# The slot tables AT, AT_FIRST and AT_LAST of a four-layer kernel laid anew

## The reference

```python
def reference(x, ...):                    # x: (16, 256, 256) float32
    # layer 0: gradients and Laplacian of each 256x256 plane with grid coefficients, an Euler step, relu
    x = _L0_cond_ref(x, A_grid, B_grid, dt)
    # layer 1: adapter 256->64, gelu, a 64x64 matrix chosen by the sequence's id, 64->256, residual, layer norm
    hidden = gelu(x @ down_W.T + down_b)
    hidden = hidden @ expert_W[id].T + expert_b[id] + domain_emb[id]
    x = layer_norm(hidden @ up_W.T + up_b + x) * ln_gamma + ln_beta
    # layer 2: scale and shift from a small network of t; norm over the whole plane, silu, 256x256 product, twice
    h = silu(noise_encoding(t) @ W1 + b1) @ W2 + b2
    scale, shift = h @ Wsc + bsc, h @ Wsh + bsh
    out = silu(scale * plane_norm(x) + shift) @ W_in + b_in
    x = silu(scale * plane_norm(out) + shift) @ W_out + b_out + x
    # layer 3: adaptive layer norm, attention of 16 heads of width 16 with bias and mask, MLP 256->1024->256
    x = ln(x) * (1 + scale3) + shift3
    probs = softmax(mask(q @ k.T / 4 + attention_bias))
    x = x + (probs @ v) @ Wo + bo
    return x + gelu2(ln(x) * g2 + beta2) @ W1 + b1) @ W2 + b2
```

## Time and profile before

| What | us |
|---|---|
| median of 3 runs | 923.07 (922.08 to 923.43) |
| the profiled execution | 923.14 |
| its span, first to last instruction | 921.10 |
| front of pair 0, until the first exponential | 84.31 |
| turn of pair 0 | 95.85 |
| turns of pairs 1 to 6, each | 104.44 to 104.79 |
| turn of pair 7 | 81.68 |
| after the start of the last head's exponential | 31.84 |

### The profile page before, as it was taken

One profiled execution on the slowest core, in us unless ns is written; L12 is line 12 of the kernel. 1 busy time (PEld: TensorE's weight loads), 2 busy tenths in 40 slices (PEclk: granted clock), 3 DMA queues, 4 the chain that ended last, 5 costly groups with the idle time before them and its releaser, 6 DMA issues.

```text
span 921.1 us, 18266 instructions
## 1 busy us (share of the span) xinstructions
PE 859.3 (93%) x5712; PEld 665.7 (72%) x5797; DVE 740.4 (80%) x2371; ACT 729.5 (79%) x1904; POOL 236.6 (26%) x236
## 2 busy tenths in 40 slices
PE   9876979999999999999999999999999999999987
PEld 8564657777777777777777777777777777777666
DVE  8767798888898888788898898788898898865542
ACT  2134879889798879979798878979798888977763
POOL 2232223332222313332123323232132323120000
PEclk9996999999999999999999999999999999999999
DMA  9827473744456453744446462744446452646400
GB/s 258 237 69 185 142 192 93 196 121 117 136 155 164 134 156 98 208 122 125 138 143 157 137 166 82 194 143 138 133 131 172 118 165 91 189 133 168 142 12 23
DMA packets 133082, 130.90 MB, mean 142 GB/s; under 512 B 18265, under 2 KB 123481, under 8 KB 132969
## 3 DMA queue, kind: packets, MB, share of 16 engines
q1 hardware_dynamic: 101616, 112.02, 42.9%
q10 hardware_dynamic: 31370, 17.71, 6.9%
HBM read 112.61 MB, written 17.07 MB: 141 GB/s over the span
## 4 chain that ended last, share of the span: by engine, by line
PE 57%; ACT 20%; DVE 8%; issue 3%; POOL 0%; ACTq 0%; DVEq 0%
PE ff_ps L1368 11%; PE ff_ps L1349 8%; PE PT_ps L1404 7%; ACT Pr L1083 5%; PE G L1154 5%; PE scores_ps L1389 4%; PE G L1146 4%; PE ctx_ps L1426 3%; DVE bias L928 3%; ACT L1083 3%; PE scores_ps L1386 2%; ACT ffT L1069 2%; ACT tanh L1065 2%; PE ff_ps L1335 2%; ACT PT L1096 2%
## 5 line engine op out<-in xcount | busy, mean ns | idle before, releaser
L1083 ACT ACTIVATE Pr<-bias,nmax 128x256 f32<-128x256 f32 x512 | 255.8, 506 | 35.3 <-DVE nmax L928 34.6
L928 DVE CUSTOM_DVE_ANT_0 bias<-scores_ps,bias 128x256 f32<-128x256 f32 x512 | 194.0, 419 | 48.2 <-PE scores_ps L1389 26.7
L1096 ACT ACTIVATE PT<-PT_ps 128x512 f32<-128x512 f32 x256 | 152.4, 596 | 50.9 <-PE PT_ps L1404 46.3
L1404 PE MATMUL PT_ps<-ident,Pr 128*128 128x128 f32 x1024 | 156.0, 274 | 7.8 <-ACT Pr L1083 7.8
L566 POOL TENSOR_TENSOR rstd<-var,half_neg 128x2 f32<-128x2 f32 (+1 forms) x64 | 43.4, 678 | 388.6 <-DVE var L691 244.5
L1404 PEld LDWEIGHTS PT_ps<-ident,Pr 128*128 128x128 f32 x1024 | 119.9, 141 | 16.6 <-ACT Pr L1083 13.0
L1349 PE MATMUL ff_ps<-ctxT,w 128*128 128x256 f32 x480 | 117.2, 387 | 13.0 <-ACT ffT L1069 10.7
L1368 PE MATMUL ff_ps<-w,ffT 128*128 128x256 f32 x480 | 113.1, 381 | 0.3 <-DVE ffT L905 0.3
L1349 PEld LDWEIGHTS ff_ps<-ctxT,w 128*128 128x128 f32 x480 | 86.3, 190 | 33.0 <-ACT ffT L1069 16.3
L1389 PE MATMUL scores_ps<-k_stack,q_stack 96*128 96x256 bf16 x512 | 99.3, 275 | 6.1 <-issue 2.1
L1083 ACT ACTIVATION_READ_ACCUMULATOR Pr<-bias,nmax 128x1 f32 x512 | 100.5, 196 | 0.0
(11 more groups left out here) (223 smaller groups left out, 1649.0 us busy)
## 6 DMA issues: line engine op xcount, KB each, us to landing
bias<-in_fside_Bx16xSxS_dram SPq DMA_DIRECT2D x256, 256.0 KB, 3.2
part_dram<-front ACTq DMA_DIRECT2D x32, 384.0 KB, 2.8
q_stack<-part_dram SPq DMA_DIRECT2D x32, 192.0 KB, 3.8
k_stack<-part_dram SPq DMA_DIRECT2D x32, 192.0 KB, 3.7
F<-in_x_dram SPq DMA_DIRECT2D x16, 256.0 KB, 3.7
ada<-rows_dram SPq DMA_DIRECT2D x16, 256.0 KB, 4.6
q_stack<-part_dram SPq DMA_DIRECT2D x32, 128.0 KB, 3.7
k_stack<-part_dram SPq DMA_DIRECT2D x32, 128.0 KB, 3.7
```

The costliest lines, as they stand in the source:

```text
L928: nc.vector.tensor_tensor_reduce(out=t, in0=SP_[:, n % 2, q * S:(q + 1) * S], in1=t, scale=-1.0, scalar=BIG, op0=ALU.add, op1=ALU.min, acc ...
L1083: ins = nc.scalar.activation(Pr[:, n % PR, q, :], bias[:, n // CH % RING, 2 * (n % CH) + q, :], ACT.Exp, bias=nmax[:, n, q:q + 1], scale=-1.0,
L1096: nc.scalar.activation(PT[:, m % BATCH, :, :].rearrange("p c q -> p (c q)"), TP[:, m % 2, :], ACT.Identity).then_inc(pt_ok, 1)
L1404: ins = pe.transpose(TP[:, m % 2, c * S + q * P:c * S + (q + 1) * P], Pr[:, m % PR, q, c * P:(c + 1) * P], ident[:, :])
```

## The change

The three tables get other numbers. No instruction is added, taken out or moved to another engine, and the loops, waits and warming products stay as they are; SP's queue is the same row by row. Most numbers of `AT` move by 0.25 to 2 slots; those of `AT_FIRST` and `AT_LAST` by up to 32. A line or two of each table:

```diff
 AT
-      "wo": (21.75, 37.25), ... "w1": ((25, 26.25, 28, 29.75), (41.75, 42.75, 43, 45.75)),
+      "wo": (21.75, 38.75), ... "w1": ((25, 26.75, 28.5, 29), (42, 43.5, 43.75, 45.75)),
-      "k_out": (28, 41.75), "v": (28.75, 46), "V": (29, 46.5), "mask": (20, 2)}
+      "kf": (25, 40.75), "k_split": (26.75, 42), "k_out": (26.5, 43.25), "v": (28.75, 43.5), "V": (30, 45.75),
 AT_FIRST
-AT_FIRST = {"s_gelu": (3.25, 3.25), ... "s_sel": (2, 2), ... "l0": (4, 8.75),
+AT_FIRST = {"s_gelu": (10.5, 10.5), ... "s_sel": (1.5, 1.5), ... "l0": (1, 11.5),
 AT_LAST
-           "w2": ((31.25, 37, 47, 48.25), (67, 73.25, 75.75, 77.5)), "out": (55.25, 70), "store": (57, 68.75)}
+           "w2": ((37.25, 40.75, 42.25, 49), (67.5, 82.25, 84.75, 90.75)), "out": (69.25, 90.75),
```

More of the change, by code:

```diff
@@ L72 @@
            "masks": 0}
-AT = {"x4": (27.75, 46.25), "ctx_spread": (19.5, 40.5), "ctx": (19.75, 36.25), "ctx_scale": (19.5, 36.25),
[4 rows of a table removed]
-      "out": (35, 51.25), "store": (36.75, 57.5), "prods_p": (0.5, 18.75), "prods": (0.75, 14), "diffs": (2, 16.5),
[8 rows of a table removed]
-      "q_split": (25.5, 40.25), "q_out": (25.25, 42), "k": (25.5, 41), "kf": (25, 40.5), "k_split": (26.75, 41.75),
-      "k_out": (28, 41.75), "v": (28.75, 46), "V": (29, 46.5), "mask": (20, 2)}
-AT_FIRST = {"s_gelu": (3.25, 3.25), "s_sin": (0.25, 0.25), "s_se": (2.75, 2.75), "s_trig": (3.5, 3.5), "s_onehot": (4, 4),
-            "s_grid": (4.25, 4.25), "s_h1": (3, 3), "s_h2": (3.5, 3.5), "s_h2t": (3.75, 3.75), "s_sel": (2, 2),
-            "s_cond": (4.5, 4.5), "s_condt": (6.25, 6.25), "s_mask": (24.25, 24.25), "s_rows": (15.25, 15.25),
-            "x4": (28, 46.75), "s_fill": (4.25, 4.25), "s_bq": (7.75, 7.75), "s_w2": (34.25, 34.25),
-            "prods_p": (0.25, 5.5), "prods": (5.5, 6), "diffs": (5.5, 6.5), "edges": (5.5, 6.5), "l0": (4, 8.75),
-            "x1": (5.75, 12), "relu": (4.25, 7), "x1_turn": (4.75, 16.5), "x1T": (5, 7.25), "res1": (5.75, 13.75),
-            "down": (6.25, 16.75), "hid": (5.75, 7.5), "expert": (6.5, 17.5), "expT": (6.5, 7.75), "up": (8.5, 18),
[7 rows of a table removed]
@@ L103 @@
-AT_LAST = {"ctx_spread": (23.25, 35.25), "ctx": (20.5, 41.25), "ctx_scale": (20.5, 38.5), "wo": (22, 46),
[4 rows of a table removed]
-           "w2": ((31.25, 37, 47, 48.25), (67, 73.25, 75.75, 77.5)), "out": (55.25, 70), "store": (57, 68.75)}
+AT = {"x4": (28.25, 51.5), "ctx_spread": (21.25, 35.5), "ctx": (20.75, 37.5), "ctx_scale": (20, 37.25),
[4 rows of a table added]
+      "w2": ((30.5, 31.5, 33.5, 35.25), (46.25, 47.75, 49.5, 51.5)), "out": (35.5, 51.75), "store": (37.25, 62),
+      "prods_p": (0.75, 20), "prods": (1.5, 13.25), "diffs": (3, 16.5), "edges": (3.25, 16.75), "l0": (5, 18.25),
+      "x1": (5.75, 18.75), "relu": (5.75, 18.75), "x1_turn": (7, 20.5), "x1T": (6, 19), "res1": (6.5, 27),
+      "down": (8.5, 21.5), "hid": (8.25, 20.5), "expert": (9.75, 21.75), "expT": (8.75, 20.5), "up": (10, 22),
[7 rows of a table added]
+      "mask": (20, 2)}
@@ new lines @@
+AT_FIRST = {"s_gelu": (10.5, 10.5), "s_sin": (0.5, 0.5), "s_se": (2.75, 2.75), "s_trig": (0.25, 0.25),
+            "s_onehot": (2.25, 2.25), "s_grid": (2.25, 2.25), "s_h1": (2, 2), "s_h2": (2, 2), "s_h2t": (2.5, 2.5),
+            "s_sel": (1.5, 1.5), "s_cond": (3.5, 3.5), "s_condt": (7.5, 7.5), "s_mask": (21.5, 21.5),
+            "s_rows": (13, 13), "x4": (21, 44), "s_fill": (7.25, 7.25), "s_bq": (24, 24), "s_w2": (35.25, 35.25),
+            "prods_p": (0.75, 0.75), "prods": (3.75, 6.25), "diffs": (3.75, 6.25), "edges": (4.5, 7.25),
+            "l0": (1, 11.5), "x1": (5.25, 12.5), "relu": (3, 6.25), "x1_turn": (3.5, 12.75), "x1T": (3.5, 11.5),
+            "res1": (0.75, 5.25), "down": (8, 13.75), "hid": (4, 17), "expert": (8, 14.75), "expT": (5, 18.25),
[8 rows of a table added]
@@ L109 @@
+AT_LAST = {"ctx_spread": (18, 37.75), "ctx": (21.25, 34.75), "ctx_scale": (21.25, 43.25), "wo": (22, 38),
[5 rows of a table added]
+           "store": (58.25, 94.25)}
 SP_AT = {"front": (0, 7), "stacks": (1, 2, 9, 11), "mask": 6, "rows": (12, 3)}
```

## The result

The changed kernel takes 931.8 us (median of 10 runs, 926.8 to 935.6), the kernel before 923.1 (10 runs beside it). The ratio is 1.0079, with a 95% interval of 1.0051 to 1.0107: it is slower by 0.8%, where 917.3 and faster was forecast. The profiled execution took 931.08 us with a span of 929.1, which is 8.0 longer than the span before; between the medians it is 8.7.

| stage | before | after | change | forecast |
|---|---|---|---|---|
| front of pair 0 | 84.31 | 93.85 | +9.54 | +7.7 |
| turn of pair 0 | 95.85 | 100.45 | +4.60 | -2.8 |
| turns of pairs 1 to 6 | 627.42 | 621.91 | -5.51 | -10.2 |
| turn of pair 7 | 81.68 | 77.88 | -3.80 | -1.0 |
| end | 31.84 | 35.01 | +3.17 | +0.5 |

What follows compares the result with a forecast made beforehand. PE was taken to bound the six steady turns, and a step-by-step sequence across engines the front of pair 0. Front +7.7, turn 0 -2.8, steady -10.2, turn 7 -1.0, end +0.5: -5.8, so 923.1 becomes 917.3 us (range 909 to 930).

Steps and rivals of the forecast that it cites:

- (D): Front of pair 0: after idling, PE runs `l0` at the low clock, 3.1 us more, total 920.4; chance 0.12.
- the slack at `xs`: Front of pair 0: `xs` waited for DVE after `up`, so 2.45 us of the 10.2 delay is taken up.
- paid on the path: Front of pair 0: the first gelu table's load of 1.28 us now follows the wait of `hid`, delaying the first sequence.
- The 1.41 before `w_out`: Turn of pair 0: PE's wait before pair 1's first-sequence `w_out` goes, as it stands two slots behind `y1`; 1.41 us.
- the 1.38: Turn of pair 0: PE's wait before the second sequence's `w_out` is half covered by two more heads; 0.69 us gained.
- DVE has the same work before it: Turn of pair 0: the reason given why the largest wait, 3.16 us for DVE's statistics, stays.
- The waits that I listed: Steady turns: PE's five waits for ACT, before `w1` (three), `turn_p` and `q`, 2.40 us together, would be covered.
- comes out of slot 14, where PE had much queued and ACT little: Steady turns: `v`, 1.73 us and no new work, moves from there between `w1` pieces and covers the 0.79 wait.
- the new waits for which I took off 0.7: Steady turns: late `x1T` on ACT and work meeting on DVE in slot 13 cut the 2.40 gain to 1.7 each.
- The bound of 3.5: Steady turns: PE's idle time, the most a new order could give back in each, in us.
- (A): Rival: the front of pair 0 costs and the steady turns give nothing, total 929.9 us; chance 0.22.
- (B): Rival: DVE's meeting in slots 13 and 16 costs another 1.0 us a steady turn, total 923.3, no change; chance 0.14.

Runs made afterwards that it cites:

- e11: The changed kernel with 78 opening products on TensorE in place of 50, order unchanged: 926.9 us.
- e5: The changed kernel with `l0` of pair 0's first sequence moved back from 1 to 3 in `AT_FIRST`, behind the setup: 920.2 us.
- e18: The changed kernel with the old `AT_FIRST` and, in the turn of pair 0, mostly the old numbers of `AT`: 920.8 us.
- e2: The kernel before with the new `AT_FIRST` alone: 938.3 us.
- e12: The kernel before with two numbers of the second sequence changed in `AT`, `v` from 46 to 43.5 and `V` from 46.5 to 45.75: 929.2 us.
- e16: The kernel before with `v` of the second sequence at 42.75 and `V` at 45.75 in `AT`: 928.0 us.
- e19: The changed kernel with old `AT_FIRST` and `AT_LAST` and, in the turn of pair 0, mostly the old numbers of `AT`: 920.9 us.

## Why the prediction was wrong

The forecast change was -5.8, the measured one +8.0 (between the profiled executions, whose stages are compared here). The gap of 13.8 is 1.8 in the front, 7.4 in the turn of pair 0, 4.7 in the steady turns and -0.1 in the last two stages.

**The front of pair 0: mechanism right, one term too small.** `x1_turn` was forecast 8.9 later and came 10.99 later: `l0`'s input was there 1.3 sooner than I assumed, and the low clock added 3.3 or more (e11). I had priced it at 3.1 from the length of `l0` and kept it as a rival (D) with 0.12. The old kernel's 0.88 was no reason against it: that clock had other places, and PE did not idle for 7.7 us there. The table load did appear (`expert` is 12.25 later, 1.26 more than `x1_turn`), and the slack at `xs` took up 2.8 where I counted 2.45 (the statistics are 9.46 later). In e5 the same load costs nothing, so "paid on the path" holds only less the slack that it shares with the delay.

**The turn of pair 0: the step that failed.** I summed three waits that would go and added none. The 1.41 before `w_out` became 1.09, and the 1.38 became 1.84. The wait for DVE's statistics fell from 3.16 to 1.88, which I had not claimed, but others came or grew: 2.00 before `expert`, 1.75 before `w_in` (0.72 before), 1.21 before `l0`. In all PE was idle for some 1.5 us more, where 2.8 less was forecast. PE's waits in this turn of the changed kernel:

```profile
101.68 3.53 PE L1157 MATMUL G<-w_out,front 128*128 128x256 f32 x8 [1.84 <-ACT front L1034]
...
120.71 0.44 PE L1262 MATMUL G<-front,ew 64*64 64x128 f32 x4 [2.00 <-ACT front L1020]
...
130.21 0.38 PE L1277 MATMUL G<-ms,mean_mat 128*128 128x2 f32 x2 [1.88 <-DVE ms L685]
...
135.56 1.99 PE L1149 MATMUL G<-front,w_in 128*128 128x256 f32 x8 [1.75 <-ACT front L1034]
...
146.35 0.70 PE L1229 MATMUL G<-front,gradT 128*128 128x256 f32 x2 [1.21 <-DVE front L798]
...
152.37 1.97 PE L1157 MATMUL G<-w_out,front 128*128 128x256 f32 x8 [1.09 <-ACT front L1034]
```

And I did not ask which work crosses the boundary of a turn: about 3.1 us (e18) that the steady turns do not show and the first turn pays. The prediction had this term at nothing. "DVE has the same work before it" was nearly true of the amount in this turn (276 instructions for 273) and not of the order.

**The steady turns: right direction, half the size.** The waits that I listed fell as foretold, 2.81 us with a 0.41 that I had missed down to 0.43, and one of 0.59 came before `w_in`. In the turn of pair 2 PE's idle time fell from 2.82 (e2's row) to 1.20, by 1.6 us, but the turn by 0.8 only: in the new order the same products keep PE busy for 102.47 in place of 101.62. The prediction put that at nothing, and the trace gives no reason for it. The failed sentence is that `v` "comes out of slot 14, where PE had much queued and ACT little": PE's queue there was what hid the wait for `y0` (e12 and e16). Of the new waits for which I took off 0.7, none at `x1T` shows among PE's rows. The bound of 3.5 was too high by 0.7, through the missing records.

**Turn 7 and the end: right together, wrong apart.** -3.80 and +3.17 make -0.63, against -0.5. The new AT takes 0.8 off the turn (e19), where 1.0 was forecast. I had put the earlier last exponential into the end: `AT_LAST` takes 3.0 us off the turn (e18 against e19) and gives them back behind the last head; e18 and e19 have the same median.

Of the rivals, (D) was true and (A) half true: the start costs, but the steady turns do gain. The case that came, a slower turn of pair 0, was none of them. (The chances do not add up as told either: with (B) alone at 0.14, "same" had to be about 0.17 with what was left of (D).)
